# Edge features and the largest zero fill moved beside the scatters of the second node map, in a graph kernel on one core

## The reference

```python
# layer 0: ten hops over the edges, row = src, col = dst
for _ in range(10):
    out = segment_sum(out[col] * w[:, None], row, N) * 0.9 + h * 0.1
...
# layer 3: every edge has a feature row made from its one weight
e = relu(edge_attr @ W_l0 + b_l0) @ W_l1 + b_l1        # (E,1) -> (E,96) -> (E,96)
msg = relu(x[src] + e)                                 # used twice
agg = segment_sum(msg, dst, N)
```

## Time and profile before

| | |
|---|---|
| median of 3 runs | 19,699.26 us (19,690.18 to 19,725.49) |
| profiled execution, its own time | 19,798.93 us |
| its span | 19,797.3 us |
| mean granted TensorE clock | 0.586 of full |
| busy share of the span | PE 21%, DVE 38%, ACT 23%, POOL 45% |
| `sort_dst` with `load_dst` | 452 to 1,241 us |
| `map_dst` with the barrier behind it | 1,242 to 1,759 us |
| `hop_second` | 2,366 to 3,143 us |

### The profile page before, as it was taken

The page is one execution under the profiler, slowest core; times in us unless marked ns, Lnnn a source line. Parts: engine busy times, 40 slices in busy tenths (PEclk is TensorE's granted clock), DMA queues, the critical chain, the costliest instruction groups (busy, mean ns, idle before and its releaser), DMA issues. The chain is left out here.

```text
span 19797.3 us, 123940 instructions
## 1 busy us (share of the span) xinstructions
PE 4154.2 (21%) x18516; PEld 3096.2 (16%) x18516; DVE 7463.9 (38%) x23392; ACT 4583.8 (23%) x13127; POOL 8959.5 (45%) x9881
## 2 busy tenths in 40 slices
PE   0000031000000000000036102555555100270078
PEld 0000031000000000000025001444444100150056
DVE  7541233333333332262159321000566741231145
ACT  0001321111111111043135222222111420130045
POOL 0736655566566666725630565444000047407710
PEclk9965555555555555555555555777777555695555
DMA  5901233333333331152135222111333531241144
GB/s 174 378 9 28 70 104 94 93 91 96 93 94 95 90 96 58 48 195 83 30 113 197 76 65 65 63 58 56 127 120 120 174 123 47 85 183 48 47 152 164
DMA packets 691059, 2030.30 MB, mean 103 GB/s; under 512 B 296971, under 2 KB 308950, under 8 KB 669412
## 3 DMA queue, kind: packets, MB, share of 16 engines
q1 hardware_dynamic: 345428, 1385.45, 20.3%
q0 software_dynamic: 329360, 564.80, 10.6%
q10 hardware_dynamic: 16128, 78.68, 1.0%
HBM read 1228.59 MB, written 839.09 MB: 104 GB/s over the span
## 5 line engine op out<-in xcount | busy, mean ns | idle before, releaser
L512 POOL DMA_INDIRECT hop_odd_raw<-hop_table,hop_odd_wanted x1176 | 1116.0, 949 | 416.4 <-issue 388.0
L512 POOL DMA_INDIRECT hop_even_raw<-hop_table,hop_even_wanted x1176 | 1113.5, 947 | 415.6 <-issue 389.6
L745 POOL DMA_INDIRECT sums<-gine_sums,gine_target x784 | 795.2, 1014 | 305.4 <-issue 278.0
L512 POOL DMA_INDIRECT cheb_raw<-cheb_table,cheb_wanted x784 | 744.1, 949 | 272.6 <-issue 263.0
L865 PE MATMUL cheb_mixing<-folded,cheb_hops_turned 96*128 96x292 f32 x2352 | 820.6, 498 | 0.0
L1502 POOL DMA_DIRECT2D mid<-cheb_nodes_rows x56 | 29.9, 533 | 1604.8 <-DVEq L1901 1604.8
L745 POOL DMA_INDIRECT mixed<-cheb_mixed,cheb_target x392 | 385.6, 984 | 759.5 <-ACT cheb_mixed L894 615.8
L569 DVE SCALAR_TENSOR_TENSOR cheb_total<-cheb_ends,cheb_joins,cheb_rows 128x96 f32<-128x96 f32 x84 | 27.3, 325 | 1840.0 <-ACT cheb_rows L612 1758.6
L1723 PE MATMUL cheb_nodes_product<-folded,cheb_nodes_turned_rows 97*128 97x292 f32 x1568 | 547.1, 499 | 693.5 <-DVE cheb_nodes_mixed L1869 590.8
L612 ACT ACTIVATE hop_odd_rows<-hop_odd_raw,hop_odd_weights 128x96 f32<-128x96 f32 x1176 | 321.0, 360 | 1522.1 <-remote 686.5
L612 ACT ACTIVATE hop_even_rows<-hop_even_raw,hop_even_weights 128x96 f32<-128x96 f32 x1176 | 321.0, 360 | 1503.5 <-remote 661.0
(11 more groups left out here) (461 smaller groups left out, 19044.2 us busy)
## 6 DMA issues: line engine op xcount, KB each, us to landing
mixed<-sort_dst_fill SPq DMA_DIRECT2D x56, 2044.0 KB
cheb_nodes_mixed<-mixed SPq DMA_DIRECT2D x56, 2044.0 KB, 9.3
gine_nodes_sums<-sums SPq DMA_DIRECT2D x112, 672.0 KB, 6.2
hop_odd_res<-hop_table SPq DMA_DIRECT2D x84, 672.0 KB
hop_table<-hop_odd_sums SPq DMA_DIRECT2D x84, 672.0 KB
hop_even_res<-hop_table SPq DMA_DIRECT2D x84, 672.0 KB
hop_table<-hop_even_sums SPq DMA_DIRECT2D x84, 672.0 KB
start_x<-x_and_map SPq DMA_DIRECT2D x56, 700.0 KB, 4.4
```

The lines of the kernel that those rows point to most:

```text
L512: pool.indirect_dma_start(out=raw_rows[:, h, g, :], out_offset=None, in_=table, in_offset=bass.IndirectOffsetOnAxis(ap=wanted[:, h, g:g + ...
L745: pool.indirect_dma_start(out=self.out, out_offset=bass.IndirectOffsetOnAxis(ap=self.target[:, h, g:g + 1], axis=0), in_=self.rows(ph, h, ...
```

## The change

`scatter_map` becomes `map_and_features`. The features are made in the phase of the second map, by the same formulas, with PE, ACT, DVE and SP running their 28 batches while POOL scatters; `hop_second` becomes a plain hop. The zero fill of `mixed` (56 stores of 2,044 KB) leaves `sort_dst` and is issued by SP in the map's phase, two stores ahead of each features store. `f_turned` gets a second PSUM tile, and PE turns quad q+1 ahead of the matmuls of quad q.

```diff
-def scatter_map(nc, k, name, maps):
+def map_and_features(nc, k, maps, features, fill):
+    with Phase(nc, "map_dst", maps.SEMS + features.SEMS + fill.SEMS) as ph:
...
         @block.gpsimd
         def _(pool):
+            fill.pool(ph, pool)
             maps.pool(ph, pool)
+        @block.sync
+        def _(sp):
+            features.sync_setup(ph, sp)
+            for b in range(2 * pairs):
+                fill.issue_part(ph, sp, b, 2 * pairs)
+                features.store(ph, sp, b, b % 2)
+            features.sync_end(ph, sp)
+            fill.wait(ph, sp)
+        @block.vector
+        def _(dve):
+            features.vector_setup(ph, dve)
+            def body(i, first, last):
+                for h in range(2):
+                    features.vector(ph, dve, i, h, first)
+            loop(dve, pairs, body)
...
+    def issue_part(self, ph, sp, part, parts):
+        if part == 0:
+            sp.wait_ge(ph.sems["fill_made"], sum(len(values) for _, values in self.fills))
+        for (table, _), (tile, per, times, _) in zip(self.fills, self.tiles):
+            for m in range(part * times // parts, (part + 1) * times // parts):
+                sp.dma_start(table[m * per * P:(m + 1) * per * P, :].rearrange("(p t) c -> p t c", p=P),
+                             tile[:, :, :]).then_inc(ph.sems["fill_stored"], 16)
+    def wait(self, ph, sp):
+        sp.wait_ge(ph.sems["fill_stored"], 16 * sum(times for _, _, times, _ in self.tiles))
...
-        self.turned = ph.psum("f_turned", [C, 4, P])
+        self.turned = [ph.psum(f"f_turned{n}", [C, 4, P]) for n in range(2)]
...
         pe.wait_ge(s["f_staged"], i * 2 + h + 1)
+        def turn(q):
+            g0, n = QUADS[q]
+            if not (first and h * 4 + q < 2):
+                pe.wait_ge(s["f_relu"], i * 8 + h * 4 + q - 1)
+            for g in range(g0, g0 + n):
+                ins = nc.tensor.transpose(self.turned[q % 2][:, g - g0, :],
+                                          self.weights[:, h, g:g + 1].to_broadcast([P, C]), self.k.ident[:, :])
+            ins.then_inc(s["f_turned"], 1)
+        turn(0)
         for q, (g0, n) in enumerate(QUADS):
             at = i * 8 + h * 4 + q
...
+            if q + 1 < len(QUADS):
+                turn(q + 1)
             pe.wait_ge(s["f_relu"], at + 1)
...
-        fills = FillRows(nc, [(hop_sums, (0.0,)), (sums, (0.0,)), (mixed, (0.0,))]
+        fills = FillRows(nc, [(hop_sums, (0.0,)), (sums, (0.0,))]
...
-        scatter_map(nc, k, "map_dst", maps_dst)
+        map_and_features(nc, k, maps_dst, Features(nc, k, W_l0, b_l0, W_l1, b_l1, feats),
+                         FillRows(nc, [(mixed, (0.0,))]))
...
-        hop("hop_second", Store(nc, k, hop_a, hop_first), hop_first, 2, k.s_second, beside=features)
+        hop("hop_second", Store(nc, k, hop_a, hop_first), hop_first, 2, k.s_second)
```

More of the change, by code:

```diff
@@ L419, in _ @@
               .then_inc(s["carried"], 1)
-def scatter_map(nc, k, name, maps):
-    with Phase(nc, name, maps.SEMS) as ph:
+def map_and_features(nc, k, maps, features, fill):
+    with Phase(nc, "map_dst", maps.SEMS + features.SEMS + fill.SEMS) as ph:
         maps.buffers(ph)
+        features.buffers(ph)
+        fill.buffers(ph)
+        pairs = k.T // (2 * GROUP)
         block = ph.block()
@@ L429, in _, with body @@
         def _(pool):
+            fill.pool(ph, pool)
             maps.pool(ph, pool)
+        @block.sync
[13 more added lines that the diff above has]
+            loop(dve, pairs, body)
+        @block.scalar
+        def _(act):
+            features.scalar_setup(ph, act)
+            def body(i, first, last):
+                for h in range(2):
+                    features.scalar(ph, act, i, h, first)
+            loop(act, pairs, body)
+        @block.tensor
+        def _(pe):
+            features.tensor_setup(ph, pe)
+            def body(i, first, last):
+                for h in range(2):
+                    features.tensor(ph, pe, i, h, first)
+            loop(pe, pairs, body)
 def edge_pass(nc, k, name, side, finish, table, index, weight=None, added=None, scale=None, fix_scale=None,
-              meets=None, beside=None):
+              meets=None):
     T = k.T
@@ L443, in edge_pass @@
             "copied", "tail", "carried", "fixed", "fix_added", "pool_own", "met", "rooted"] + finish.SEMS
-    sems += beside.SEMS if beside else []
     width = table.shape[1]
@@ L476, in edge_pass @@
         finish.buffers(ph, k)
-        if beside:
-            beside.buffers(ph)
         block = ph.block()
@@ L482, in _ @@
         def _(sp):
-            if beside:
-                beside.sync_setup(ph, sp)
             def body(i, first, last):
                 for h in range(2):
-                    if beside:
-                        beside.sync(ph, sp, i, h, first)
                     if added is not None:
@@ L497, in _ @@
             finish.sync_end(ph, sp)
-            if beside:
-                beside.sync_end(ph, sp)
         @block.gpsimd
@@ L571, in body @@
                         finish.vector(ph, dve, i, h, q, g0, n, first)
-                    if beside:
-                        beside.vector(ph, dve, i, h, first)
-            if beside:
-                beside.vector_setup(ph, dve)
             loop(dve, pairs, body, own)
@@ L582, in body @@
                     finish.tensor(ph, pe, i, h, first)
-                    if beside:
-                        beside.tensor(ph, pe, i, h, first)
-            if beside:
-                beside.tensor_setup(ph, pe)
             loop(pe, pairs, body)
@@ L615, in body @@
                     finish.scalar(ph, act, i, h, first)
-                    if beside:
-                        beside.scalar(ph, act, i, h, first)
-            if beside:
-                beside.scalar_setup(ph, act)
             loop(act, pairs, body)
@@ L1179, in store @@
         sp.dma_start(self.out[:, bass.ds(b * GROUP, GROUP), :], self.made[:, h, :, :]).then_inc(ph.sems[f"f_stored{h}"], 16)
-    def sync(self, ph, sp, i, h, first):
-        if not (first and h == 0):
-            self.store(ph, sp, i * 2 + h - 1, 1 - h)
     def sync_end(self, ph, sp):
-        self.store(ph, sp, 2 * self.pairs - 1, 1)
         for h in range(2):
@@ L1216, in scalar @@
                 act.wait_ge(s["f_product"], at - 1)
-            self.nc.scalar.activation(self.hidden[:, q % 2, 0:n, :], self.turned[:, 0:n, :], ACT.Relu,
+            self.nc.scalar.activation(self.hidden[:, q % 2, 0:n, :], self.turned[q % 2][:, 0:n, :], ACT.Relu,
                                       bias=self.c0[:, 0:1], scale=self.w0[:, 0:1]).then_inc(s["f_relu"], 1)
@@ L1225, in tensor @@
         pe.wait_ge(s["f_staged"], i * 2 + h + 1)
+        def turn(q):
[7 more added lines that the diff above has]
+        turn(0)
         for q, (g0, n) in enumerate(QUADS):
             at = i * 8 + h * 4 + q
-            if not (first and h == 0 and q == 0):
-                pe.wait_ge(s["f_relu"], at)
-            for g in range(g0, g0 + n):
-                ins = nc.tensor.transpose(self.turned[:, g - g0, :], self.weights[:, h, g:g + 1].to_broadcast([P, C]),
-                                          self.k.ident[:, :])
-            ins.then_inc(s["f_turned"], 1)
+            if q + 1 < len(QUADS):
+                turn(q + 1)
             pe.wait_ge(s["f_relu"], at + 1)
@@ L2130, in graph_layers @@
         load_side(nc, k, by_dst, ordered_dst, 1, k.edge_weight)
-        scatter_map(nc, k, "map_dst", maps_dst)
+        map_and_features(nc, k, maps_dst, Features(nc, k, W_l0, b_l0, W_l1, b_l1, feats),
+                         FillRows(nc, [(mixed, (0.0,))]))
         prepare(nc, k, by_src, by_dst)
-        features = Features(nc, k, W_l0, b_l0, W_l1, b_l1, feats)
         def hop(name, into, table, n, scale, index=k.i_hop, **more):
```

## The result

| | us |
|---|---|
| before, median of 4 runs | 19,703.25 (19,690.18 to 19,725.49) |
| after, median of 4 runs | 19,841.10 (19,834.77 to 19,892.12) |
| ratio, with its 95% interval | 1.0074 [1.0055, 1.0094] |
| profiled execution of after, its own time and span | 19,834.77 and 19,833.1 |

The change costs 137.9 us on the medians, where 137 were predicted. The stretches of the changed kernel are, in this order, the whole map phase, its scatters, two pieces of what follows them, and the second hop; the columns are those of the earlier trace rows.

The account below looks back on a forecast made before the run. Barriers make the kernel a sum of phases, with engines beside POOL's indirect DMAs held by late reports. Map phase +301, second hop -156.6, second sort -7 gave 137 us more: 19,837 us, range 19,660 to 19,940.

Parts of the forecast that it names:

- The theory of late reports: Beside POOL's indirect DMAs, instructions run on time but completions are reported late, 1.37 us for each LDWEIGHTS and MATMUL.
- 17.5 free reports: Beside POOL's indirect DMAs, about 17.5 completion reports go through before the engine feels the delay.
- The map phase: Phase of the second map, taking in features and fill: 819 us against 517.7, 301 us more.
- Scatters: POOL's 392 scatters in the map's phase, taken at 515 us, bounds 509.5 and 533.2.
- Batches done in time: Feature batches PE gets reported during the map phase's 515 us of scatters: 4.7.
- Tail: After the map phase's scatters, 23.3 batches left at 12.7 us each, limited by the DMA engines: 296 us.
- The hop: Second hop, rid of the features, becomes like the mean plain hop: 776.3 to 619.7 us, 156.6 us off.
- The second sort: Sort losing the 56 fill stores: scatters and memset end sooner, DVE leaves its slow pace earlier, 7 us off.
- Third rival: The fill makes the second sort slow: 116 us off instead of 7, so 19,728 us; chance 0.07.
- The 99.7 us: Whole kernel: the profiled execution stands 99.7 us above the median of the runs, a difference taken to stay.
- The first rival: Map phase: PE isn't held beside these scatters, all batches fit under them, 143 us gained: 19,556 us; chance 0.12.
- The second: Rival: the delay belongs to the profile's recording and is absent from timed runs: 19,692 us, no change; chance 0.09.

Follow-up runs that it names:

- the window: Changed kernel, its map-phase scatters in parts of 7, POOL waiting only for the part before the last: 17,936.0 us, 1.0010 of the kernel before.

## Why the prediction was right, point by point

**The theory of late reports** is shown as far as the sum needs it. Work without scatters isn't late, the lateness goes by the number of PE's instructions (84 and 44, both at 1.400 us; I had 1.37 from two turns), and full waits of POOL end it. Two steps of the argument were wrong without harm. POOL does pause in this phase, three times, but such a pause gives nothing back. And the 17.5 free reports are no constant, as the next point shows. What the trace of before couldn't show is that the delay isn't there on every chip; whether the chip, its host or the way it is recorded makes the difference, no run tells.

**The map phase** grew by 299 us against 301, with errors that cancel. Scatters: 523 us, not 515. Batches done in time: the sixth was stored 26 us after the last scatter, so that at the last scatter 5.7 were done instead of 4.7. The cause is the start: by 1649.24 five batches, 420 reports, were stored, 440.9 us after the first scatter, in which 1.400 us each allow 315. So 105 reports had gone through free, not 17.5 (69 with the features alone); the relus show prompt reports up to 1223, 15 us after the first scatter, and a late one at 1235.86. Tail: 22 batches in 242.4 us, 11.0 each against 12.7. I took 384 GB/s for the full DMA engines; they gave 426, 11.7 us a batch, and the first nine intervals had PE's 10.0. Then 20 us from the last store to `prepare`, for which I had 3.

**The hop** lost 149.6 us against 156.6. The size isn't firmer than some 26 us: with the features in it the second hop took 776.3, 756.8 and 750.2 us in three executions on chips that hold up, without them 620.5 to 626.7.

**The second sort** gave 38 us in the profile against 7, and no run shows that this is the change's: seven executions without the fill end it anywhere from 1186 to 1222. Third rival, the fill as the cause of the slow sort: out, since in the changed kernel DVE is busy for 158.5 of 285 us (0.56) from 700 to 985, beside scatters with the DMA engines at 0.02, and full waits free the sort with the other fills still in it.

**The 99.7 us** between the profiled execution of before and its median didn't stay. Stated against one profiled execution the sum would have been 19,936; that of after took 19,834.8. The execution before was long in parts that the change doesn't touch: from the last hop's start to the end 12,316.3 us, against 12,234 to 12,302 in the ten later traces with the delay. Median against median, 137.9 us stand for the sum of 137. That I took the difference off both sides gave the right figure; the sentence that it stays was wrong. And the agreement to a microsecond is luck: the same two kernels lay 178.3 us apart on the second chip, and between the two profiled executions the three terms of the sum come to 299.3 - 149.6 - 38.4 = 111, not 137.

**The first rival** (PE not held, 19,556) is the case on the third chip in its mechanism, and its price falls there: the same absence of delay empties the gain in the hop. Both terms of the sum, +301 and -157, came from one delay that the third chip doesn't have, and I had varied it in only one of them. **The second,** that timed runs have no delay, is out in the form that I gave it. The Trainium skill, NOTIFIC — the notification-queue block, section 7.1, says that inside the block which writes the records a pipeline always holds back rather than lose one. No run here shows that this block is the cause; the third chip, recorded in the same way, held back nothing.

## What to carry to other kernels

Before work is put beside a long run of indirect DMAs, count its instructions, LDWEIGHTS too, and look in the trace for how late their completion is seen; engines that look idle there may take 1.4 us for each. Where that is so, let POOL wait for all its DMAs after every 14: that freed a sort for 152 us or more, less 37 for the waits. But try it on more than one chip: on one that doesn't delay, such waits in both maps cost 0.9%, and the move that this document is about, with the window, only 0.1%.

## What the runs showed that I had not expected

- The interval of the reports is 1.400 us in all six traces with features beside unbroken scatters on chips with the delay, whatever the load of the DMA engines (0.04 or 0.15) and whether the batch has 84 or 44; DVE, alone in the sort, runs at the same 1.400.
- One chip of the four has no such delay at all, and runs the same kernel in 17,927 instead of 19,700 us, though its gathers and scatters take as long as on the others (medians of 948 and 977 ns, against 948 and 977 to 980).
- A full wait after 14 scatters is worth nearly everything, even one of 1.9 us. A stop of POOL of 2.9 to 7.1 us without such a wait is worth nothing, and a window of up to 14 scatters never made POOL wait.
- In the same features, PE's granted clock rose from 0.50 to 1.00 (10 us a batch became 6.1) without the fill, and in one of two traces of the changed kernel, for two batches, with it.
